# Four graph layers on one core: weight preparation moved to other places and engines, and spare TensorE products of 128 columns

## The reference

```python
# layer 0
e = leaky_relu((x @ W1) @ (x @ W2).T);  a = softmax(where(adj > 0, e, -1e12));  relu(a @ (x @ W3))
# layer 1
h = x @ W;  e = leaky_relu(h @ a1 + (h @ a2).T);  elu(softmax(where(adj > 0, e, -9e15)) @ h)
# layer 2
out = relu(x @ mlp1 + b1);  out = elu(gat(out, None, W_fc, a_fc)) + out
out = relu(out @ mlp2 + b2);  out = elu(gat(out, adj, W_hand, a_hand)) + out;  relu(out)
# layer 3: four heads
q, k, v = x @ wq.T + bq, x @ wk.T + bk, x @ wv.T + bv
softmax(where(adj == 0, -inf, q k.T / 8)) v @ wo.T + bo
```

## Time and profile before

| | |
|---|---|
| median of 3 runs | 2616.76 us (2615.21 to 2622.59) |
| profiled execution, its own time | 2616.98 us |
| its span, first to last instruction | 2615.2 us |
| mean granted clock of TensorE | 0.988 |
| busy: PE, PEld | 2525.4 us (97%), 2411.0 us (92%) |
| busy: DVE, ACT, POOL | 2251.1 (86%), 1968.4 (75%), 1913.2 us (73%) |
| instructions | 64667 |

### The profile page before, as it was taken

How to read it: one execution, slowest core, us unless ns; L and a number is a source line. 1 busy time by engine, 2 the same in 40 slices (tenths; PEclk the granted TensorE clock), 3 DMA queues, 4 the chain that set the end, 5 groups by cost and what they waited for, 6 DMA issues and landing times. The chain is left out here.

```text
span 2615.2 us, 64667 instructions
## 1 busy us (share of the span) xinstructions
PE 2525.4 (97%) x21399; PEld 2411.0 (92%) x21399; DVE 2251.1 (86%) x6252; ACT 1968.4 (75%) x4737; POOL 1913.2 (73%) x2439
## 2 busy tenths in 40 slices
PE   6899999999999999999999999999999999999886
PEld 5789999999999999999999999999999999999874
DVE  2478999899999998999999999999989999998874
ACT  2468877887887788778778877877887788787652
POOL 2457877877787877778787777878777787877543
PEclk8899999999999999999999999999999999999998
DMA  4214444444444444444444444344444444443333
GB/s 141 67 52 128 129 142 130 126 139 130 136 123 145 127 126 142 129 138 121 145 126 130 139 134 133 124 142 128 131 134 136 132 128 141 128 132 110 105 106 89
DMA packets 317115, 329.67 MB, mean 126 GB/s; under 512 B 35313, under 2 KB 248689, under 8 KB 316785
## 3 DMA queue, kind: packets, MB, share of 16 engines
q1 hardware_dynamic: 316784, 325.54, 41.5%
HBM read 174.41 MB, written 150.99 MB: 124 GB/s over the span
## 5 line engine op out<-in xcount | busy, mean ns | idle before, releaser
L1234 POOL TENSOR_TENSOR p<-p,rd 128x512 f32<-128x512 f32 x256 | 343.1, 1350 | 5.5
L1159 POOL TENSOR_TENSOR proT_lo<-sco,proT_hi 128x512 fp32r<-128x512 f32 x128 | 165.8, 1295 | 159.7 <-ACT proT_hi L560 159.7
L1171 POOL TENSOR_SCALAR xn<-act,nmean,rstd 128x256 f32<-128x256 f32 x384 | 237.1, 627 | 47.7 <-DVE act L1075 35.3
L786 ACT ACTIVATE p<-p,nmx 128x256 f32<-128x256 f32 x512 | 253.0, 496 | 10.9 <-DVE nmx L1109 10.9
L573 ACT ACTIVATE sco<-sco,nmax 128x256 f32<-128x256 f32 x384 | 192.6, 502 | 40.9 <-DVE nmax L872 36.1
L1181 POOL TENSOR_TENSOR act<-act,x 128x512 f32<-128x512 f32 x64 | 82.9, 1295 | 167.8 <-ACT act L623 167.8
L1109 DVE CUSTOM_DVE_ANT_0 p<-ps,mask 128x256 f32<-128x256 f32 x512 | 188.3, 414 | 15.4 <-PE ps L510 14.0
L872 DVE CUSTOM_DVE_ANT_0 sco<-ps,mask 128x256 f32<-128x256 f32 x384 | 144.9, 414 | 53.2 <-ACT ps L563 41.2
L808 DVE TENSOR_TENSOR xnT_lo<-ps,xnT_hi 128x512 fp32r<-128x512 f32 x192 | 129.7, 675 | 61.0 <-ACT xnT_hi L560 61.0
L1166 POOL TENSOR_TENSOR rstd<-vare,mhalf 128x2 f32<-128x2 f32 x256 | 178.1, 696 | 0.0
L1124 DVE STREAM_TRANSPOSE p<-p 128x1024 f32<-128x1024 f32 x128 | 158.6, 1239 | 18.0 <-POOL p L1234 17.7
(11 more groups left out here) (240 smaller groups left out, 12396.6 us busy)
## 6 DMA issues: line engine op xcount, KB each, us to landing
scratch<-p SPq DMA_DIRECT2D x128, 512.0 KB, 3.0
p4T<-scratch SPq DMA_DIRECT2D x512, 128.0 KB, 3.5
scratch_pro<-act SPq DMA_DIRECT2D x192, 256.0 KB, 2.3
sco<-scratch_pro SPq DMA_DIRECT2D x768, 64.0 KB, 1.9
x0Tp<-in_xT SPq DMA_DIRECT2D x64, 256.0 KB, 2.6
x<-in_x SPq DMA_DIRECT2D x64, 256.0 KB, 2.8
scratch_o<-sco SPq DMA_DIRECT2D x64, 256.0 KB, 2.1
o3r<-scratch_o SPq DMA_DIRECT2D x256, 64.0 KB, 2.5
```

Source lines behind the costliest of these rows:

```text
L786: ins = nc.scalar.activation(rows_, rows_, ACT.Exp, scale=-1.0, bias=nmx4[:, h, m:m + 1], accum_out=den4[:, h, m:m + 1])
L1159: return G.tensor_tensor(lo, whole, hi.bitcast(fp32), ALU.subtract)
L1171: ins = G.tensor_scalar(xn[:, m, :], y[:, m, :], nmean[i][:, m:m + 1], rstd[i][:, m:m + 1], ALU.add, ALU.mult)
L1234: G.tensor_tensor(rows_, rows_, rd4[:, h, :].unsqueeze(2).unsqueeze(3).broadcast_to([P, NT, QUADS, CT * QP]), ALU.mult).then_inc(S["p4n"], 1)
```

## The change

- **Spare products** multiply `ones2` (128 x 128, ones, fp32r) by itself instead of W3's part: 128 columns instead of 256. `ones2` is now filled by GpSimd at the start. Their numbers change: opening 95 to 77, and 14 more before the A0 product and 8 behind it (`busy`); filling 52 to 185; closing 188 to 694.
- **Loads**: the first group is only W1T and W2T; W3 and adj come behind the first x0T, under a semaphore of their own (`loaded4`). The head weights (8 transfers) are issued after the x0T of element 1, not with the others.
- **Start on VectorE**: A0 is split first, then W3, then the mask.
- **Columns on TensorE**: `graph_columns` now has those of W_, hand and mlp2 and stands before g0:1; `mixed_columns` has those of fc and stands before a0:0.
- **Splits on VectorE**: made_hidden before g0:1, made_mlp1 before h0:1, made_fc before x0:1, made_mlp2 before x0:2. Before h3:0 only the mask work (`head_masks`) is left.
- **Head weights**: ScalarE makes the scaled wq and the four high parts before its a0:0 (`heads_high`), GpSimd the four low parts, two before its a0:0 and two before its l0:2 (`heads_low`).
- `run` takes the element into account in the table of what stands before a step.

```diff
-SPARE_OPENING = "h0:0:4 s0:0:3 g0:1:17 a0:0:7 h0:1:4 s0:1:4 x0:0:4 h1:0:15 h0:2:3 s0:2:3 x0:1:4 h0:3:3 s0:3:3 m2:0:16 a1:1:5"
-SPARE_FILLING = "r2:0:5 s0:4:3 m2:1:2 d2:0:11 m2:2:2 f3:0:29"
-SPARE_CLOSING = "m3:-5:2 x1:-3:2 a3:-5:2 m3:-4:2 x1:-2:2 a3:-4:11 x1:-1:2 r2:-1:6 m3:-2:7 s40:-3:3 a3:-2:17 m3:-1:17 s40:-2:3 s42:-2:5 a3:-1:19 a4:-2:25 s40:-1:1 s42:-1:5 a4:-1:52 y4:-1:5"
+SPARE_LOADING = 14
+SPARE_OPENING = "h0:0:6 s0:0:6 h0:1:6 s0:1:5 x0:0:6 h1:0:6 h0:2:5 s0:2:5 x0:1:6 h0:3:5 s0:3:5 m2:0:8 a1:1:8"
+SPARE_FILLING = "r2:0:20 s0:4:16 m2:1:11 d2:0:37 m2:2:11 f3:0:90"
+SPARE_CLOSING = "m3:-5:12 x1:-3:11 a3:-5:29 m3:-4:12 x1:-2:11 a3:-4:38 m3:-3:12 x1:-1:11 r2:-1:24 m3:-2:26 s40:-3:15 a3:-2:55 m3:-1:61 s40:-2:15 s42:-2:20 a3:-1:49 a4:-2:88 s40:-1:11 s42:-1:20 a4:-1:154 y4:-1:20"
...
-        LOADS = (("W1T", "W2T", "W3"), ("W_T", "a1", "W_"), ("mlp1", "b1", "afc", "mlp2", "b2", "hand", "hand_T", "ahand", "m1"), ("wqT", "bq", "wkT", "bk", "wvT", "bv", "woT", "bo"))
+        LOADS = (("W1T", "W2T"), ("W_T", "a1", "W_"), ("mlp1", "b1", "afc", "mlp2", "b2", "hand", "hand_T", "ahand", "m1"), ("wqT", "bq", "wkT", "bk", "wvT", "bv", "woT", "bo"))
...
             def later_weights():
-                sp.dma_start(adj_sb, adj).then_inc(S["loaded0"], 16)
+                sp.dma_start(W["W3"], weights["W3"]).then_inc(S["loaded4"], 16)
+                sp.dma_start(adj_sb, adj).then_inc(S["loaded4"], 16)
...
                 load_weights(2)
-                load_weights(3)
...
                 if t == 0:
                     later_weights()
+                if t == 1:
+                    load_weights(3)
...
+            def busy(b, count):
+
+                for _ in range(count):
+                    nc.tensor.matmul(ps[:, b, 0:P], ones2[:, :], ones2[:, :], start=True, stop=True)
+
+            pe.wait_ge(S["setup_pool"], 2)
+            busy(4, SPARE_LOADING)
             pe.wait_ge(S["loaded0"], 16 * n_loads[0])
...
             ins.then_inc(S["setup_pe"], 1)
+            busy(4, 8)
             pe.wait_ge(S["made"], 1)
...
-                for _ in range(count):
-                    nc.tensor.matmul(ps[:, b, 0:N], WP["W3"][0][:, 0, 0:P], WP["W3"][0][:, 1, :], start=True, stop=True)
+                busy(*spare.get((name, t), (0, 0)))
...
-                {"a0": graph_columns, "h1": made(2), "a1": mixed_columns, "m2": made(3), "n2": made(3), "c2": made(4), "m3": made(5), "q4": made(6), "k4": made(6), "v4": made(6)}, keep_busy)
+                {("h0", 0): made(2), ("g0", 1): graph_columns, ("a0", 0): mixed_columns, ("h1", 0): made(3), ("m2", 0): made(4), ("n2", 0): made(4), ("c2", 0): made(5), ("m3", 0): made(6),
+                 ("q4", 0): heads_made, ("k4", 0): heads_made, ("v4", 0): heads_made}, keep_busy)
...
+            def heads_high():
+                ac.wait_ge(S["loaded3"], 16 * n_loads[3])
+                nc.scalar.activation(W["wqT"], W["wqT"], ACT.Copy, scale=QSCALE).then_inc(S["heads_h"], 1)
+                ac.wait_ge(S["heads_h"], 1)
+                for n in HEAD_WEIGHTS:
+                    copy(WP[n][0][:, :, :], W[n]).then_inc(S["heads_h"], 1)
...
-                {"x0": made_hidden, "h1": made_mlp1, "x1": made_fc, "c2": made_mlp2, "h3": made_heads})
+                {("g0", 1): made_hidden, ("h0", 1): made_mlp1, ("x0", 1): made_fc, ("x0", 2): made_mlp2, ("h3", 0): head_masks})
...
+            def heads_low(i):
+
+                def step():
+                    for k in (i, i + 1):
+                        n = HEAD_WEIGHTS[k]
+                        po.wait_ge(S["heads_h"], k + 2)
+                        low_part(WP[n][1][:, :, :], W[n], WP[n][0][:, :, :]).then_inc(S["heads"], 1)
+                return step
```

More of the change, by code:

```diff
@@ L43, in run @@
                     ahead(name, k - s)
-                if k == s and name in before:
-                    before[name]()
+                if (name, k - s) in before:
+                    before[name, k - s]()
                 steps[name](k - s)
@@ L90, in graph_stack @@
         WIDE = {"W_": [P, CT, C2], "hand": [P, CT, C2], "fc": [P, HT, H2 + 2]}
+        HEAD_WEIGHTS = ("wqT", "wkT", "wvT", "woT")
         SPLIT = ("fc", "mlp1", "mlp2", "wqT", "wkT", "wvT", "W3", "W_", "hand", "woT")
@@ L174, in graph_stack @@
         bank = [ps[:, b, :].rearrange("p (m n) -> p m n", m=2) for b in range(8)]
-        names = """loaded0 loaded1 loaded2 loaded3 made wsplit setup_pe setup_dve setup_pool
+        names = """loaded0 loaded1 loaded2 loaded3 loaded4 heads_h heads made wsplit setup_pe setup_dve setup_pool
  x0T_in x0_in x0Th x0Tl g0_mm g0h g0 h0_mm h0h h0 s0_mm raw0 nmax0 pro0 rden0 pro0_x pro0_dma proT0h proT0 av0_mm act0 y0 mv0 rstd0
@@ L208, in graph_stack @@
         scratch_o3 = nc.dram_tensor("scratch_o3", [P, QUADS, CT * N // QUADS], fp32, kind="Internal").ap()
-        LOADS = (("W1T", "W2T", "W3"), ("W_T", "a1", "W_"), ("mlp1", "b1", "afc", "mlp2", "b2", "hand", "hand_T", "ahand", "m1"), ("wqT", "bq", "wkT", "bk", "wvT", "bv", "woT", "bo"))
-        n_loads = [len(LOADS[0]) + 1, len(LOADS[1]) + 1, len(LOADS[2]) + 2 + HT, len(LOADS[3])]
+        LOADS = (("W1T", "W2T"), ("W_T", "a1", "W_"), ("mlp1", "b1", "afc", "mlp2", "b2", "hand", "hand_T", "ahand", "m1"), ("wqT", "bq", "wkT", "bk", "wvT", "bv", "woT", "bo"))
+        n_loads = [len(LOADS[0]), len(LOADS[1]) + 1, len(LOADS[2]) + 2 + HT, len(LOADS[3])]
         @block.sync
@@ L333, in graph_columns @@
                     for k in range(CT):
-                        ins = nc.tensor.matmul(bank[6][:, m, 0:2], W["W_T"][:, k, m * P:(m + 1) * P], W["a1"][:, k, :], start=(k == 0), stop=(k == CT - 1))
-                ins.then_inc(S["setup_pe"], 1)
-            def mixed_columns():
+                        nc.tensor.matmul(bank[6][:, m, 0:2], W["W_T"][:, k, m * P:(m + 1) * P], W["a1"][:, k, :], start=(k == 0), stop=(k == CT - 1))
                 pe.wait_ge(S["loaded2"], 16 * n_loads[2])
-                pe.wait_ge(S["setup_pool"], 1)
                 for m in range(CT):
@@ L342, in mixed_columns @@
                         nc.tensor.matmul(bank[7][:, m, 0:2], W["hand_T"][:, k, m * P:(m + 1) * P], W["ahand"][:, k, :], start=(k == 0), stop=(k == CT - 1))
-                for m in range(HT):
-                    for k in range(HT):
-                        nc.tensor.matmul(bank[5][:, 0, 2 * m:2 * m + 2], fcT_tiles[k][:, m * P:(m + 1) * P], W["afc"][:, k, :], start=(k == 0), stop=(k == HT - 1))
                 for m in range(CT):
@@ L349, in mixed_columns, with heads_made @@
                 ins.then_inc(S["setup_pe"], 1)
+            def mixed_columns():
+                for m in range(HT):
+                    for k in range(HT):
+                        ins = nc.tensor.matmul(bank[5][:, 0, 2 * m:2 * m + 2], fcT_tiles[k][:, m * P:(m + 1) * P], W["afc"][:, k, :], start=(k == 0), stop=(k == HT - 1))
+                ins.then_inc(S["setup_pe"], 1)
             def made(n):
                 return lambda: pe.wait_ge(S["made"], n)
+            def heads_made():
+                pe.wait_ge(S["heads"], 4)
             tenants = {}
@@ L800, in _ @@
                        "q4": q4, "k4": k4, "p40": p4_(0), "p41": p4_(1), "p42": p4_(2), "p43": p4_(3),
-                       "a4": a4}, B)
+                       "a4": a4}, B, {("a0", 0): heads_high})
         @block.vector
@@ L824, in whole_weight @@
                 return (WP[n], slice(0, W[n].shape[1]), slice(0, W[n].shape[2]), W[n])
-            dv.wait_ge(S["loaded0"], 16 * n_loads[0])
-            V.tensor_scalar(mask16[:, :, :], adj_sb, 0.0, MASK, ALU.is_le, ALU.mult)
-            split([whole_weight("W3")])
             dv.wait_ge(S["setup_pe"], 1)
@@ L832, in _ @@
             split([(A0, slice(0, CT), slice(0, C), A0f[:, :, :])]).then_inc(S["made"], 1)
+            dv.wait_ge(S["loaded4"], 32)
+            split([whole_weight("W3")]).then_inc(S["made"], 1)
+            V.tensor_scalar(mask16[:, :, :], adj_sb, 0.0, MASK, ALU.is_le, ALU.mult)
             def made_hidden():
@@ L843, in made_fc @@
             def made_fc():
-                dv.wait_ge(S["setup_pool"], 1)
                 dv.wait_ge(S["setup_pe"], 3)
-                V.tensor_copy(ones2[:, :], ones[:, 0:1].broadcast_to([P, P]))
                 places = [(WP["fc"], slice(0, HT), slice(C, C2), bank[5][:, 0, 0:2 * HT].rearrange("p (m c) -> p m c", c=2))]
@@ L855, in made_mlp2, with head_masks @@
                 split([whole_weight("mlp2"), whole_weight("hand"), (WP["hand"], slice(0, CT), slice(C, C2), bank[7][:, :, 0:2])]).then_inc(S["made"], 1)
-            def made_heads():
+            def head_masks():
                 dv.wait_ge(S["loaded3"], 16 * n_loads[3])
@@ L861, in made_heads @@
                 V.tensor_scalar(bq8[:, :], W["bq"][:, :, 0], QSCALE, None, ALU.mult)
-                V.tensor_scalar(W["wqT"], W["wqT"], QSCALE, None, ALU.mult).then_inc(S["setup_dve"], 1)
+                ins.then_inc(S["setup_dve"], 1)
                 dv.wait_ge(S["setup_dve"], 2)
@@ L866, in made_heads @@
```

(4 more changed lines are left out.)

3 lines of the change are left out of this document (1 added, 2 removed).

## The result

2624.92 us, median of 9 runs (2622.04 to 2626.15), against 2617.01 for the kernel before in runs beside it: ratio 1.0025, interval 1.0015 to 1.0036. That is 0.25% slower, clear of the noise but within the 0.3% called "no change"; 2622 was forecast. The medians are 7.9 apart.

What follows compares the result with a forecast made beforehand. TensorE's own work bounds 165 to 2385 us, untouched; opening and closing are a chain through all engines. Terms 12.2 + 3.7 - 6 - 5.0 + 1.3 + 1.1 + 0 - 2.6 = +4.7 gave 2622 us against 2617, range 2603 to 2648.

Steps and rivals of the forecast that it cites:

- Price of a spare product, 0.112 us: New 128-column fp32r spare products on TensorE: paced by the weight load, 0.112 us each, bounds 0.06 and 0.23; 48%.
- the rival "cheap": Spare products cost 0.06 to 0.085 us, so the closing adds nothing: 2603 to 2611 us; 33%.
- The fallback rival: fp32r falls back at 128 columns to 0.2 to 0.23 us a product: about 2710 us; 11%.
- a clock that falls in the fill: Spare products at 0.112 us do not hold TensorE's clock: 2635 to 2655 us; 8%.
- Closing +12.2: Closing, 2385 to 2607 us: 694 spare products take 77.7 us in waits of 64, overruns add: +12.2 us.
- clock -6: Filling and closing: denser spare products win back two thirds of 9 us lost to half clock: -6 us (0 to -9).
- +3.7 said: Filling, r2:0 to f3:0: 185 spare products take 20.7 us in waits of 17 us: +3.7 us.
- Start -5.0: Kernel start: new load order and A0 split first bring the first g0 at 8.5 to 10 us: -5.0 us.
- Head loads +1.3: SP's queue: eight head-weight loads between x0T(1) and the first pro_out delay what waits behind: +1.3 us (0 to +2).
- ScalarE's heads_high +1.1, GpSimd absorbed: Opening: 2.8 us on ScalarE ahead of act(0) costs +1.1 us; GpSimd's low parts make x0:0 1.7 late, absorbed.
- made_fc -2.6: VectorE, opening: made_fc no longer ahead of xnT_lo, now before x0:1: -2.6 us (-4.4 to -2).
- the terms say -5.2: Opening edits together, as the prediction's terms for the opening give them: -5.2 us.

Runs made afterwards that it cites:

- e4: Kernel before plus nine blocks of 60 products behind its last step, as a price list: fp32r, 128 weight and 128 moved columns, 0.111 us each.
- e6: Changed kernel, same counts, but spare products of filling and closing load 64 weight columns in place of 128: 2614.79 us, ratio 0.9983.
- e8: e2 with the split of the four head weights back on VectorE ahead of h3:0: 2614.05 us, ratio 0.9982.
- e10: e2 run once more on another chip, as the run beside which others stand: 2606.83 us, ratio 0.9967.
- e12: e2 with VectorE's splits of fc and mlp2 at their old places, ahead of x1:0 and c2:0: 2609.76 us, ratio 0.9971.
- e2: Changed kernel with the old counts and old 256-column spare products in filling and closing: 2608.24 us, ratio 0.9961.
- e5: Changed kernel with fewer spare products in filling and closing, 443 in the closing: 2613.34 us, ratio 0.9982.
- e7: Changed kernel with no spare products in the closing: 2619.21 us, ratio 1.0006.
- e11: e2 with all head-weight work (loads, high and low parts) moved out of the opening to later steps: 2611.64 us, ratio 0.9985.

## Why the prediction was right

The mechanism held: spare products of 0.112 us, waits overfilled one after another, and gains in the opening and by the clock that do not make up for it. That the sum also came within 3 us of the median is in part luck, as the last terms below show.

- **Price of a spare product, 0.112 us.** Measured 0.112 and, apart, 0.111. The argument from the 192 ns load held: e4 shows the pace flat from 64 to 192 moved columns, e6 halves it with the weight columns. The Trainium skill's "TensorE: Matmul & The Clock Gate", section "Back-to-back issue gap", gave 81 ns for 128 columns with their load and 56 alone; no fp32r block with 128 weight columns here shows either. The bf16 block shows 56 with the load; its load record is 98 ns long, the fp32r one 192. At the bf16 price of 0.056 the rival "cheap" would have had its condition, which is under 0.092; no kernel with bf16 spares was run. The fallback rival (0.23) and the one of a clock that falls in the fill are excluded by the same spacing and by the clock of 1.00.
- **Closing +12.2, clock -6 over both stretches.** The closing's waits grew by 13.8 and its own products shrank by 7.1; the filling's waits grew by 4.3 (+3.7 said) and its products shrank by 3.9. So the clock gave back 11.0, where I allowed 6 and at most 9: this is the term most off, by 5.0. Its working was also wrong in itself. 18 us of half clock, a third of them in products, lose 3 us and not 6, since a product at half clock lasts twice as long (0.213 us for 0.112 in e4) and loses half of that; a gain of 7.1 means that about 14 us of the half clock lay in products. The two errors partly cancel.
- **Start -5.0.** g0:0 at 9.89 (8.5 to 10 said), and s0:0 at 16.11 in place of 21.12: -5.0.
- **Head loads +1.3.** gT_hi starts 8.8 us behind the end of VectorE's transpose, 6.1 before, so +2.6 there; a0:0 is 3.6 earlier than before, so 1.4 of the lead is lost. Right in the sum.

SP's queue of the changed kernel, against the earlier trace rows; the eight loads sit between x0T and pro_out:

```profile
17.83 0.33 SPq L237 DMA_DIRECT2D x0Tp<-in_xT  x1
18.20 0.43 SPq L220 DMA_DIRECT2D p<-in_wqT  x1
...
21.53 0.44 SPq L220 DMA_DIRECT2D w_bo<-in_bo  x1
22.02 0.43 SPq L256 DMA_DIRECT2D scratch_pro<-act  x1
```

- **ScalarE's heads_high +1.1, GpSimd absorbed.** s0:1 lost 0.9 of its lead, x0:0 another 1.5 (46.20 before, 44.94 after), which I had called absorbed: GpSimd's second low part took 2.25 us, not 1.3, beside the split of mlp1 that the change moved to the same place on VectorE (last section). By m2:0 no loss is left to see in e8 against e10 (89.7 and 89.3, from s0:0 at 15.8 and 16.5: the kernel without that work takes 1.0 longer to get there, so the 1.1 is not confirmed).
- **made_fc -2.6.** m2:0 is 5.2 earlier than before where a1:0 was 2.0 earlier: -3.2. At c2:0 only 3.2 of 5.2 is left, and e12 shows about 1.4 as what such a gain keeps of its 2.8.
- **Opening in all:** the terms say -5.2. The seven kernels with the changed opening reach c2:0 at 101.5 to 104.7 (mean 103.2), the three with the old one at 104.7 to 107.7 (mean 106.1): -2.9. Among the seven it moves by 3 us; the granted clock from 20 to 40 and 40 to 60 us is 0.74 and 0.83 in the changed kernel's trace and 0.62 and 0.69 in that of e2, the latest of them. One trace doesn't price the opening better.
- **The sum.** +4.7 said; against the terms the opening gave 2.0 less (-3.2 for -5.2), the clock 5.0 more, the waits cost 2.2 more (13.8 + 4.3 for 12.2 + 3.7), and 1.2 came in between c2:3 and c2:60, where the traces of all kernels here lie between 2168.0 and 2170.5: 4.7 + 2.0 - 5.0 + 2.2 + 1.2 = 5.1, the difference of the two profiled executions. That 4.7 and 5.1 are so close is luck: the clock's error of 5.0 is made up for by those of the opening, the waits and the middle. By the medians the change costs 7.9, so there the sum is 3.2 short; single runs of one kernel spread from 2611.6 to 2626.6.
- **What I undervalued:** the head weights' move. I saw that it shortens f3:0's wait and dropped it because TensorE stood in 90 products. True for this kernel, but it is the change's best part, 4 us (e8), and the 90 products hide it.

Left open: why the closing of e5 is some 3 us longer than that of e2 at no lower a clock. Also what takes the clock of e5 and e6 down in the closing. In both traces TensorE stood idle around the last fall (for 1.60 us, to 2596.55, in e5, whose clock fell at 2597.6; for 3.80 us, to 2596.91, in e6, whose clock fell at 2595.0), while 0.84 us is the longest idle time in the changed kernel's closing; but in e4 the clock fell with no idle time at all, in the 64-column block, so idle time alone doesn't explain every fall. And a place for the eight loads where nothing is late behind them was not found.

The best version found is e2, the edits with the old spare tables: 0.9961 and 0.9967 of the kernel before.

## What to carry to other kernels

Price a filler by what it costs in place, load included, and don't let its count outlast the wait: one too many in each wait adds up through a written order, and here 694 fillers paid 13.8 us for 7.1 of clock. Ending in time is not enough to gain, either: 443 fillers that mostly end in time (e5) were slower than the old 188, and none at all cost about as little. Ask of every filled wait whether another edit has just shortened it, since the filler then hides that edit's gain. A load moved out of one transfer's way stands in another's: look at what is behind it in its queue at the new place.

## What the runs showed of the hardware that was not expected

- fp32r products with 128 weight columns cost 0.111 us from 64 to 192 moved columns and 0.120 at 256; bf16 ones 0.056 at 128 and 0.109 at 256 (e4).
- In an unbroken run of products the clock went to 0.50 during those with 64 moved columns and was back at 1.00 during those with 256 (e4).
- A closing with no spare product, its clock at 0.85 (e7), was 0.9 us longer than that of the kernel before, at 0.96 with 188 of them, and at most 2.7 us longer than in any trace with 188.
- GpSimd and VectorE held each other up when both subtracted tiles that lie in SBUF. GpSimd and VectorE, changed kernel:

```profile
36.77 1.30 POOL L1176 TENSOR_TENSOR w_wqT_lo<-p,w_wqT_hi 128x512 fp32r<-128x512 f32 x1 [4.94 <-ACT w_wqT_hi L572]
36.87 2.28 DVE L839 TENSOR_TENSOR w_mlp_lo<-o1T,w_mlp_hi 128x1024 fp32r<-128x1024 f32 x1
38.03 2.25 POOL L1176 TENSOR_TENSOR w_wkT_lo<-p,w_wkT_hi 128x512 fp32r<-128x512 f32 x1
```

The first of the two started ahead of VectorE's and took its usual 1.30. VectorE's subtraction took 2.28 where the same one took 1.23 in the kernel before, with GpSimd idle:

```profile
51.32 1.23 DVE L820 TENSOR_TENSOR w_mlp_lo<-o1T,w_mlp_hi 128x1024 fp32r<-128x1024 f32 x1
```

From GpSimd's end at 38.07 to VectorE's at 39.15 are 1.1 us, and from there to the end of GpSimd's second, 40.28, another 1.1: each looks as if it had begun its work when the other's was done. The three durations are the same to 0.02 us in the eight other traces that have these parts in this place. In e11, where the two parts run at 111 us with nothing like it on VectorE beside them, they take 1.30 and 1.28. Further on, GpSimd's fourth part isn't held up, beside a VectorE subtraction that takes one of its sources from PSUM:

```profile
46.08 1.26 POOL L1176 TENSOR_TENSOR w_woT_lo<-p,w_woT_hi 128x512 fp32r<-128x512 f32 x1
46.27 0.69 DVE L827 TENSOR_TENSOR xnT_lo<-ps,xnT_hi 128x512 fp32r<-128x512 f32 x1 [0.52 <-ACT xnT_hi L572]
```

No run was made for this alone. It puts about 1.0 us of delay on GpSimd's part and what stands behind it, where the prediction counted 2.6 us for the two low parts; VectorE's split is held up in that place in any case (2.18 in e8, which has no head weights on GpSimd, beside GpSimd's residual sum).
